# Cross-attention of a gated decoder stack: probabilities with keys on the partitions, from a pass that only finds row maxima

## The reference

```python
nx = _ln(x, g_ln2, b_ln2)
q = _heads(nx @ W_cq + b_cq, B)
k = _heads(img @ W_ck + b_ck, B)
v = _heads(img @ W_cv + b_cv, B)
s = jnp.einsum('bhqd,bhkd->bhqk', q, k) * SCALE
p = jax.nn.softmax(s, axis=-1)
co = _merge(einsum('bhqk,bhkd->bhqd', p, v), B) @ W_co + b_co
x = x + co
nx = _ln(x, g_ln3, b_ln3)
ff = jax.nn.gelu(nx @ W_ff1 + b_ff1, approximate=False) @ W_ff2 + b_ff2
x = x + ff
```

## Time and profile before

| | us |
|---|---|
| median of three runs | 491.4 |
| lowest, highest | 486.12, 491.94 |
| the profiled execution | 489.61 |
| its span, first to last instruction | 487.7 |
| mean granted TensorE clock of the profiled execution | 0.851 |

### The profile page before, as it was taken

How to read it: one execution, slowest core, us unless ns; L and a number is a source line. 1 busy time by engine, 2 the same in 40 slices (tenths; PEclk the granted TensorE clock), 3 DMA queues, 4 the chain that set the end, 5 groups by cost and what they waited for, 6 DMA issues and landing times.

```text
span 487.7 us, 6630 instructions
## 1 busy us (share of the span) xinstructions
PE 355.8 (73%) x2483; PEld 210.6 (43%) x2483; DVE 265.9 (55%) x675; ACT 201.7 (41%) x314; POOL 106.2 (22%) x144
## 2 busy tenths in 40 slices
PE   1987600996048899999998799987954998578810
PEld 1766500895024233333323476644643435456810
DVE  5245500232375998888831587536189566541157
ACT  2212200322022157777787377654442564725100
POOL 2000078000762351111110000000000235603163
PEclk9999555899566799999999599996975998989975
DMA  4493012111217466000000000007995476310232
GB/s 107 154 309 110 0 48 95 38 34 45 61 47 191 121 181 144 1 2 2 2 3 0 0 1 0 2 0 241 362 292 146 156 250 198 109 44 17 51 81 60
DMA packets 34002, 45.21 MB, mean 93 GB/s; under 512 B 4889, under 2 KB 19744, under 8 KB 33972
## 3 DMA queue, kind: packets, MB, share of 16 engines
q1 hardware_dynamic: 31156, 37.50, 26.2%
q0 software_dynamic: 2816, 7.31, 5.7%
HBM read 31.92 MB, written 12.71 MB: 92 GB/s over the span
## 4 chain that ended last, share of the span: by engine, by line
PE 59%; DVE 16%; issue 7%; ACT 6%; POOL 6%; DMA 3%; another core or an unknown queue 2%; SPq 1%; POOLq 0%; DVEq 0%; ACTq 0%
PE ps L1323 8%; PE ps L1520 6%; PE ps L1491 5%; PE ps L1508 5%; PE ps L1767 3%; PE ps L1438 3%; DVE mcol L1134 3%; PE ps L1450 3%; PE ps L1612 3%; POOL R L519 3%; PE ps L1793 2%; PE ps L1717 2%; POOL disp_d L514 2%; PE ps L1660 2%
## 5 line engine op out<-in xcount | busy, mean ns | idle before, releaser
L1134 DVE TENSOR_REDUCE mcol<-ps 128x1 f32<-128x512 f32 x128 | 80.3, 684 | 6.7 <-PE ps L1491 6.4
L686 ACT ACTIVATE R<-ps 128x1024 f32<-128x1024 f32 x64 | 62.6, 1020 | 25.2 <-PE ps L1508 24.3
L1323 PE MATMUL ps<-ident,R 128*77 128x128 f32 (+1 forms) x216 | 32.4, 289 | 27.4 <-DMA R<-disp_d 24.7
L1491 PE MATMUL ps<-R 72*128 72x512 bf16 x128 | 47.1, 399 | 1.0
L1323 PEld LDWEIGHTS ps<-ident,R 128*77 128x77 f32 (+1 forms) x216 | 25.3, 151 | 44.5 <-DMA R<-disp_d 25.1
L1508 PE MATMUL ps<-R 75*128 75x512 bf16 x128 | 37.6, 379 | 0.3 <-ACT R L686 0.2
L576 POOL DMA_INDIRECT R<-h_d,srow x16 | 16.0, 1002 | 84.3 <-DMA h_d<-ff 76.8
L1323 PE MATMUL ps<-ident,xn 128*128 128x128 f32 x48 | 12.9, 406 | 28.8 <-issue 18.0
L1520 PE MATMUL ps<-R,vaug 128*9 128x512 f32 x256 | 33.5, 595 | 0.6 <-ACT R L686 0.6
L1491 PEld LDWEIGHTS ps<-R 72*128 72x128 bf16 x128 | 12.8, 100 | 36.1 <-DVE mcol L1134 24.7
L1092 DVE TENSOR_SCALAR R<-ps,vcol 128x256 f32<-128x256 f32 x16 | 7.0, 479 | 38.4 <-PE ps L1438 38.4
(11 more groups left out here) (308 smaller groups left out, 695.6 us busy)
## 6 DMA issues: line engine op xcount, KB each, us to landing
R<-in_L_ffn_W_dram SPq DMA_DIRECT2D x1, 6144.0 KB, 19.8
h_d<-R SPq DMA_DIRECT2D x12, 256.0 KB, 2.9
q_d<-R SPq DMA_DIRECT2D x24, 96.0 KB, 2.0
R<-k_d SPq DMA_DIRECT2D x24, 96.0 KB
R<-q_d SPq DMA_DIRECT2D x8, 288.0 KB
R<-in_L_ffn_w_dram SPq DMA_DIRECT2D x1, 2048.0 KB, 11.5
h_d<-ff SPq DMA_DIRECT2D x6, 256.0 KB, 2.7
y_d<-R SPq DMA_DIRECT2D x10, 128.0 KB, 1.8
```

Source lines behind the costliest of these rows:

```text
L686: s.activation(probs[idx % 4], ps[:, 2 * (idx % 2):2 * (idx % 2) + 2, :].rearrange("p b t -> p (b t)"), ACT.Exp, scale=QK_SCALE).then_inc( ...
L1134: v.tensor_reduce(mcol[:, u, col:col + 1], bank(ring_bank("row", n)), AX.X, ALU.max).then_inc(s1_max, 1)
L1323: return m.transpose(dst, src, ident[0:k, 0:k])
L1491: m.matmul(bank(ring_bank("row", n)), Q9[0:KQ, b, h, t * P:(t + 1) * P], K9[0:KQ, b, h, :], start=True, stop=True).then_inc(s1_mm, 1)
```

## The change

Scores are computed twice. In pass one they have queries on the partitions as before, but only their maxima are taken (`cross_max`, one reduction a unit). The products of a unit are now cut to the 32 dimensions of their group of heads: two products of 32 contracted rows, on row groups 32·hg, into banks 4 and 5 or 6 and 7 in turn. Between units 1 to 10 stands an idle product of 256 columns, `spin(256)`. For each batch `split_maxima` turns the negated maxima into three bf16 parts, `max_rows` transposes them with an identity (four bf16 products), and ScalarE copies them to `cmrow`.

Pass two works in 8 quads, q = 4·b + j: head j of each of the four groups, all 512 queries of the batch. `cross_keys` makes four fp32 products, keys on the partitions and 512 queries in the columns, each on its own row group and into its own bank, and adds the negated maxima of the row with four bf16 products with a selector, `part_sel`. The pairs of banks are 0, 2, 0, 2 for the first two quads and then 4, 0, 2 in rotation. ScalarE takes the exponential straight from PSUM into `PT`, two banks at a time; `cross_values`, the copy, the output transposes and the division follow per quad, with the heads in another order (`across`). The 128 transposes of exponentials, the 32 copies and the 16 subtractions are gone.

The lists are interleaved anew. TensorE: units 0 to 10, maxima of batch 0, quad 0, units 11 and 12, quad 1, units 13 to 15, quad 2, values 0, maxima of batch 1, values 1, and then quads, values and output transposes in turn; projection 0 stands ahead of quad 7; the first feed-forward layer of batch 0 stands ahead of attention transposes and projection of batch 1. ScalarE: `evac_attnT(0, 1)` stands ahead of `std_of(3, 1, [0])`; in the end `evac_oT` and `evac_xT` of batch 0 stand ahead of `evac_attnT(1, 1)`, and two Gelus ahead of `evac_xT` of batch 1. GpSimd builds the selector and a bf16 identity behind its work for self-attention. W1 is loaded once the last values product of self-attention is done, W2 once the last one of cross-attention is. Bank numbers of the joints change with `at`.

The removed bodies of `cross_exp`, of `cross_values` and of the loops over units are those printed above; the rest of the core:

```diff
-        qcT = r1(16384 + 2048, 1024)
-        PT = [r1(8192 * b, 8192, J).rearrange("p (h t) -> p h t", h=NH) for b in range(B)]
-        PC = 8 * J
-        pc = [r1(16384 + PC * i, PC).rearrange("p (h j) -> p h j", h=8) for i in range(3)]
+        qcT = r1(22528, 1024)
+        PT = [r1(12288 + 2048 * i, 2048, J).rearrange("p (g t) -> p g t", g=4) for i in range(3)]
+        cmparts = r1(20480, 512).bitcast(BF16).rearrange("p (b t c) -> p b t c", b=B, t=TB)
+        cmrow = r1(20992, 512).bitcast(BF16).rearrange("p (b q) -> p b q", b=B)
+        part_sel = r1(21504, 2 * J).bitcast(BF16).rearrange("p (j n) -> p j n", j=4)
+        ident_b = r1(21664, P // 2).bitcast(BF16)
+        cmax = r1(21728, T * NH).rearrange("p (t h) -> p t h", t=T)
+        crest = r1(21856, TB * NH).rearrange("p (t g j) -> p t g j", t=TB, g=4)
+        sel_col = r1(21920, 4)
...
+        cross_order = [("nat", un) for un in range(11)] + [("max", 0), ("pair", 0), ("pair", 1)]
+        cross_order += [("nat", 11), ("nat", 12), ("pair", 2), ("pair", 3), ("nat", 13), ("nat", 14), ("nat", 15)]
+        cross_order += [("pair", 4), ("pair", 5), ("max", 1)] + [("pair", p) for p in range(6, 4 * HG)]
+        cross_done = {use: i + 1 for i, use in enumerate(cross_order)}
+        pair_bank = lambda p: (0, 2)[p % 2] if p < 4 else (4, 0, 2)[(p - 4) % 3]
+        score_bank = lambda un: 4 + 2 * (un % 2)
+        max_of = lambda un: un + 1 + un // T
+        parts_of = lambda b: (T + 1) * (b + 1)
...
-            sp.wait_ge(o_norm, 4 * HG)
+            sp.wait_ge(pv_mm, TB * UNITS)
             sp.dma_start(W1, a["L1_ffn_W1"].rearrange("e m h -> m e h")).then_inc(ld_W1, 16)
+            sp.wait_ge(c_pv, 2 * HG)
             sp.dma_start(W2, a["L1_ffn_W2"].rearrange("e (k f) m -> f (e k) m", f=P)).then_inc(ld_W2, 16)
...
-            pool.wait_ge(c_mm, 2 * T)
+            pool.wait_ge(part_wr[0], 64 * B)
+            pool.wait_ge(part_wr[1], 64 * (HG - 1) * B)
+            me.step(g.memset(r1(20480, 512), 0.0))
+            me.step(g.tensor_copy(ident_b, ident[:, :]))
+            me.link(g.memset(sel_col, 0.0))
+            for i in range(3):
+                for hg in range(HG):
+                    me.link(g.affine_select(out=sel_col, in_=sel_col, compare_op=ALU.not_equal, fill=1.0,
+                                            base=-(32 * hg + 4 * i), pattern=[[-1, 4]], channel_multiplier=1))
+            g.tensor_copy(part_sel, sel_col.unsqueeze(2).to_broadcast([P, 4, J])).then_inc(kbd_ready, 1)
+            pool.wait_ge(c_mm, len(cross_order))
...
-            evac_attnT(0, 0)
+            evac_attnT(0, 0, 0)
+            evac_attnT(0, 1, 1)
             std_of(3, 1, [0])
-            evac_attnT(0, 1)
...
+            def evac_max_rows(b):
+                act.wait_ge(c_mm, cross_done["max", b])
+                s.copy(cmrow[:, b, :], bank((0, 7)[b])).then_inc(c_row, 1)
+            def cross_exp(q, half):
+                act.wait_ge(c_mm, cross_done["pair", 2 * q + half])
+                if q >= 3 and half == 0:
+                    act.wait_ge(c_pv, q - 2)
+                bk = pair_bank(2 * q + half)
+                s.activation(PT[q % 3][:, 2 * half:2 * half + 2, :].rearrange("p g t -> p (g t)"),
+                             ps[0:J, bk:bk + 2, :].rearrange("p b t -> p (b t)"), ACT.Exp, scale=QK_SCALE).then_inc(c_exp, 1)
+            evac_max_rows(0)
+            for q in range(2 * HG):
+                cross_exp(q, 0)
+                if q >= 1:
+                    evac_oT(2 * HG + q - 1, c_pv, q)
+                cross_exp(q, 1)
+                if q == 2:
+                    evac_max_rows(1)
+                if q == 5:
+                    evac_attnT(1, 0, 7)
             std_of(4, 1, [0])
-            evac_attnT(1, 1)
+            evac_oT(4 * HG - 1, c_pv, 2 * HG)
+            evac_xT(4, V_LN3, [0], (4, 5))
+            evac_attnT(1, 1, 7)
...
-            evac_xT(4, V_LN3, [0])
             std_of(4, 1, [1])
-            for f in range(3):
+            for f in range(2):
                 gelu(0, f)
-            evac_xT(4, V_LN3, [1])
-            gelu(0, 3)
+            evac_xT(4, V_LN3, [1], (4, 5))
+            for f in range(2, 4):
...
+                heads = attn[:, b * TB:(b + 1) * TB, :].rearrange("p t (g j d) -> p t g j d", g=4, j=4)
+                v.tensor_tensor(heads[:, :, :, hg, :] if across else heads[:, :, hg, :, :],
...
-            for un in range(2 * T):
-                dve.wait_ge(c_mm, un + 1)
-                bk = 2 * (un % 2)
+            def cross_max(un):
+                t, half = un // 2, un % 2
+                dve.wait_ge(c_mm, cross_done["nat", un])
+                bk = score_bank(un)
                 sc = ps[:, bk:bk + 2, 0:4 * J].rearrange("p b (h j) -> p b h j", h=4)
...
+                v.tensor_reduce(cmax[:, t, 8 * half:8 * half + 8].rearrange("p (b h) -> p b h", b=2), sc, AX.X,
+                                ALU.max).then_inc(c_max, 1)
+            def split_maxima(b):
+                dve.wait_ge(kbd_ready, 2)
+                dve.wait_ge(c_max, max_of(T * (b + 1) - 1))
+                top = cmax[:, b * TB:(b + 1) * TB, :].rearrange("p t (g j) -> p t g j", g=4)
+                cols = cmparts[:, b].rearrange("p t (g c) -> p t g c", g=4)
+                me.link(v.tensor_scalar(cols[:, :, :, 0:4], top, -1.0, None, ALU.mult))
+                me.link(v.scalar_tensor_tensor(out=crest, in0=top, scalar=-1.0, in1=cols[:, :, :, 0:4], op0=ALU.mult,
+                                               op1=ALU.subtract))
+                me.link(v.tensor_copy(cols[:, :, :, 4:8], crest))
+                v.tensor_tensor(cols[:, :, :, 8:12], crest, cols[:, :, :, 4:8], ALU.subtract).then_inc(c_max, 1)
+            for un in range(T):
+                cross_max(un)
+            split_maxima(0)
+            for un in range(T, 2 * T):
+                cross_max(un)
+            split_maxima(1)
+            for j in range(HG):
+                normalize(2 * HG + j, j, 0, across=True)
+            normalize(3 * HG, 0, 1, across=True)
+            add_projection(1, 0, 6)
             stats_of_sum(1, 0)
-            for hg in range(2, HG):
-                normalize(3 * HG + hg, hg, 1)
+            normalize(3 * HG + 1, 1, 1, across=True)
             scale_of(xa, xn, 4, 0)
-            add_projection(1, 1)
+            for j in range(2, HG):
+                normalize(3 * HG + j, j, 1, across=True)
+            add_projection(1, 1, 6)
...
+            def group_rows(hg):
+                return slice(32 * hg, 32 * hg + 32)
             def cross_scores(un):
                 t, half = un // 2, un % 2
+                if un == 0:
+                    pe.wait_ge(qc_ready, 1)
+                elif un == T:
+                    pe.wait_ge(qc_ready, 2)
                 if un >= 2:
-                    pe.wait_ge(c_sub, un - 1)
-                else:
-                    pe.wait_ge(qc_ready, un + 1)
+                    pe.wait_ge(c_max, max_of(un - 2))
                 for j in range(2):
-                    h = 8 * half + 4 * j
-                    ins = m.matmul(ps[:, 2 * (un % 2) + j, 0:4 * J], qcT[:, t * P:(t + 1) * P],
-                                   kbd[:, t // TB, h:h + 4, :].rearrange("p h j -> p (h j)"), start=True, stop=True)
+                    hg = 2 * half + j
+                    ins = m.matmul(ps[:, score_bank(un) + j, 0:4 * J], qcT[group_rows(hg), t * P:(t + 1) * P],
+                                   kbd[group_rows(hg), t // TB, 4 * hg:4 * hg + 4, :].rearrange("p h j -> p (h j)"),
+                                   start=True, stop=True)
                 ins.then_inc(c_mm, 1)
...
+            def max_rows(b):
+                pe.wait_ge(c_max, parts_of(b))
+                if b == 0:
+                    pe.wait_ge(qc_ready, 2)
+                for s in range(TB):
+                    ins = m.matmul(ps[:, (0, 7)[b], s * P:(s + 1) * P], cmparts[:, b, s, :], ident_b, start=True, stop=True)
+                ins.then_inc(c_mm, 1)
+            def cross_keys(q):
+                b, j = q // HG, q % HG
+                if q == 1:
+                    pe.wait_ge(c_exp, 2)
+                elif q == 2:
+                    pe.wait_ge(c_max, max_of(2 * T - 2))
+                    pe.wait_ge(c_exp, 3)
+                elif q >= 3:
+                    pe.wait_ge(c_exp, 2 * q - 1)
+                banks = [pair_bank(2 * q + hg // 2) + hg % 2 for hg in range(HG)]
+                if q == 0:
+                    pe.wait_ge(c_row, 1)
+                for hg in range(HG):
+                    m.matmul(ps[0:J, banks[hg], :], kbd[group_rows(hg), b, 4 * hg + j, :],
+                             qcT[group_rows(hg), b * SEQ:(b + 1) * SEQ], start=True, stop=False)
+                pe.wait_ge(c_row, b + 1)
+                for hg in range(HG):
+                    ins = m.matmul(ps[0:J, banks[hg], :], part_sel[group_rows(hg), j, :], cmrow[group_rows(hg), b, :],
+                                   start=False, stop=True)
```

(61 more changed lines are left out.)

115 lines of the change are left out of this document (26 added, 89 removed).

## The result

The changed kernel takes 508.1 us (median of 4 runs, 506.5 to 508.7); the kernel before, run beside it, 490.3 us (4 runs, 486.1 to 491.9). The ratio is 1.037, interval 1.030 to 1.045: slower by some 18 us, and outside the range that the prediction gave. The profiled execution has a span of 504.6 us (before 487.7) and a mean granted clock of 0.814. Some executions of these kernels fall into a slower state with a lower granted clock; ratios and intervals leave them out.

The account below looks back on a forecast made before the run. It took the kernel to be TensorE bound, 1.91 us a unit. The sum - 3.3 + 3.1 + 1.5 + 0.8 = + 2.1 us on the median of 491.4 gave 493 us, with an 80% range of 483 to 504.

Parts of the forecast that it names:

- the prediction's walk: Queue-by-queue timing from entry to the second feed-forward product: start at 344.6 us against 347.93 before, 3.3 us earlier.
- the clock terms: Low-clock additions: + 3.1 us for the first layer, + 1.5 before the second, + 0.8 for quad 2's holes.
- The entry: Before the scores: ScalarE's second attention copy ahead of the variance wait starts scores at 277.9 us, 1.2 earlier.
- Row groups overlap: Scores: products on separate row groups run side by side, a quad 1.35 us; the no-overlap rival, 518 us, had chance 0.08.
- The unit at full clock: Pass one: TensorE needs 0.73 us a unit and VectorE 0.83, so VectorE bounds it.
- a change of tiling mode: Pass one, counter-argument: full-row idle products drain the array; at 0.1 us each, units take 0.93 us, ending 1 us later.
- The hole in quad 2: TensorE idles twice around quad 2, 1.5 and 2.4 us, waiting on round trips and ScalarE's queue.
- The exit: Last output transposes at 327.3 us to second feed-forward product at 344.6; first layer now precedes the second half's projection.
- the stage gains nothing that matters: Whole stage: the longer exit chain cancels the gain, a loss of 1 to 3 us; this was the forecast, chance 0.56.
- W1, W2 and GpSimd: The earlier W1 load, W2's new wait and GpSimd's sixteen set-up operations were all priced at nothing.
- the sum's term for the clock in the stage: Quad 2's holes may drop the clock: at most 3.1 us at one in four, booked as 0.8 us.
- the clock stays low in the stage: Rival: partly idle array and holes keep 1.2 GHz for five to seven quads, + 14 to + 20, 507 to 513; chance 0.12.

Follow-up runs that it names:

- g2: Changed kernel without idle products; third to eleventh units of pass one issue two extra unread products on the other two row groups; ratio 1.018.
- g3: f4 with g2's extra products on the other two row groups in place of the idle products in pass one; ratio 0.989.
- e5: Kernel before with only ScalarE's second attention copy moved ahead of its wait for the variance; ratio 1.001.
- e2: Changed kernel without the 256-column idle products between the units of pass one; ratio 1.022.
- e4: Changed kernel with the old exit order: second half's attention transposes and projection ahead of the first layer, ScalarE's order to match; ratio 1.021.
- f1: Changed kernel with the edits of e3, e4 and e6 together; ratio 1.004 to the kernel before.
- f4_w1_late: f4 with the W1 load waiting again for the last division of cross-attention, as in the kernel before; ratio 0.998.
- e1: Changed kernel with pass one's score products contracting all 128 rows again instead of 32; ratio 1.028.
- e3: Changed kernel with two 512-column idle products between units of pass one instead of one of 256; ratio 1.019.
- e6: Changed kernel with ScalarE's copy of the second batch's maxima moved ahead of the second exponential of quad 1; ratio 1.034.
- h1: g1 with every unit up to the eleventh on row groups 0 and 1 only, which alters the output; ratio 1.042.
- g1: Changed kernel without idle products; third to eleventh units of pass one issue their two row-tiled products twice, copies unread; ratio 1.018.
- g4: f4 with eleven more 512-column idle products in the holes of the exit; ratio 0.993.
- f4: f1 plus last output copy before Sqrt table load, last divisions before scaling, first output transposes before second values; 1.000. Variants: no idle products, late W1.

## Why the prediction was wrong, point by point

On the scale of the profiled executions, the prediction's walk beside the changed kernel and beside g2 and g3:

| step | forecast | changed | g2 | g3 |
|---|---|---|---|---|
| scores start | 277.9 | 278.00 | 277.97 | 278.51 |
| first quad | 290.6 | 294.45 | 289.67 | 290.23 |
| fourth quad | 306.0 | 312.06 | 304.54 | 302.37 |
| eighth quad | 319.6 | 329.65 | 319.32 | 316.65 |
| last output transposes | 327.3 | 337.02 | 326.70 | 322.97 |
| first layer | 329.2 | 339.68 | 329.27 | 328.13 |
| second layer | 340.9, 344.0 with + 3.1 | 353.59 | 343.25 | 333.19 |
| second feed-forward product | 344.6, 350.0 with the clock terms | 359.14 | 348.86 | 336.73 |

**Right.** *The queues.* With the clock up in pass one (g2), every step of the walk up to the first layer came within 1.5 us, and the second feed-forward product at 348.9 where the walk with its clock terms said 350.0. *The entry*: 278.00 for 277.9, with 0.8 to 0.9 us of gain for 1.2 (e5) that can't be seen in the time. *Row groups overlap*: the eight fp32 records of a quad take 0.92 us (303.96 to 304.88), 3.7 times less than 8 x 0.43; the whole quad 1.24 us to the next block, forecast 1.35. *The unit at full clock*: 0.93 us (280.25 to 281.18) where the forecast had 0.83, bound by VectorE. The prediction names 0.93 too, for a change of tiling mode at 0.1 us each, but that figure was met by luck: the products take 0.72 us, not 0.52 to 0.62, and take 0.7 in e2 as well, where no full-row product stands between; the idle product takes the other 0.21. *The hole in quad 2*: 1.3 and 2.1 us for 1.5 and 2.4. *The exit*: 22.1 us from the last transposes, forecast 17.3 and 4.6 for the clock. Its order was rightly seen as a loss, and e4 and f1 price it at 6.3 and 4.7 us; I booked it as "the stage gains nothing that matters", where it is a quarter to a third of the slowdown. *W1, W2 and GpSimd* at nothing: f4_w1_late bears out W1; W2 and GpSimd were not tried by themselves.

**Wrong: the clock in the stage.** The step that failed is the sum's term for the clock in the stage: 0.8 us, all of it for the holes in quad 2, and nothing for pass one behind its first two units, which was costed at the full clock at 0.83 us a unit. The runs show a unit of 1.65 us at the low clock, and 9.7 us by the last output transposes. The rival "the clock stays low in the stage" had a chance of 0.12, with 507 to 513 us, and its signs came: four quads at 2.0 us and reductions 1.65 us apart. That the median of 508 lies in its range is partly luck, though: it had 14 to 20 us for low-clock quads alone, where pass one and the quads together lost 10, and nothing for the 5.7 us at the end. The chain of the miss, in microseconds of the changed kernel over the forecast: first quad + 3.9; first to fourth quad 17.6 for 15.4, + 2.2; fourth to eighth 17.6 for 13.6, + 4.0; behind that - 0.3. That is 9.7 at the last output transposes, less the 0.8 booked, and + 0.2 in the exit: 9.1 of the 14.8 us by which the span of 504.6 misses the forecast of 489.8 (487.7 + 2.1). g2, where four row groups work in pass one, has its last output transposes 10.3 us sooner. Two causes lie in this. The first two steps, + 3.9 and + 2.2, are the low clock that pass one brings about. The + 4.0 is the dip behind the hole ahead of the fourth quad, the very place of the 0.8 us: 3.1 us at one in four, and it came. It does not hang on pass one alone. Behind the same 2.1 us hole it lasts ten microseconds in the changed kernel, in e2 and in e1, which had full rows and the full clock, and 3 to 4 in e3 and g2; with a shorter hole it is 3 to 4 us in e6 and absent in f1. What sets its length was not settled.

Two arguments carried the error. First, as evidence against the rival I took the values block at 299.40, nine output columns wide and at full clock. But it uses all four column groups and its neighbours were full-array transposes; pass one uses two row groups of four and only a short full-row product between. Nothing in the trace of before was like that, and I let the nearest row decide the chance rather than hold it as unknown. Second, I looked for the cause of a low clock in holes, since both dips of before stood behind holes. Pass one has a gap of only 0.1 us a unit by the prediction's own figures, so it seemed safe. e1, g2 and h1 show that a busy TensorE is not enough.

A smaller one: the idle product was costed at full clock, 0.11 us; at the low clock it is 0.39 with its tail and, as e2 against the changed kernel shows, 0.3 us a unit in the pace.

**Not foreseen: 5.7 us behind the second feed-forward product.** From its start to the end it is 145.5 us, and 139.8 in the trace of before. Much of this need not be the change's: the kernel before shows 142.9 and 143.5 in two other traces. Where a trace of before was taken on the same chip, the changed kernel has 144.7 beside 142.9, and h1 144.6 beside 143.5: 1 to 2 us. In g1, g3, g4 and e1 to e4, on the chips where the kernel before is at 483 us, it is 137.7 to 138.8, in g2, on the same chip as g3, 141.7. Within these kernels it is 140.7 in f1 and 143.6 to 143.9 in the three f4 ones. Low-clock stretches lie at other places there in each trace (the changed kernel: 371 to 388, 419 to 423, 429 to 436, 449 to 456). TensorE runs the same 1097 products there and is busy for 96.1 us in the changed kernel, 91.3 in the trace of before and 93.2 in its two others, so the clock has a part in it; but g3, with 93.1, has 137.7 us where the kernel before with 93.2 has 142.9. The early W1 load is not the reason (f4_w1_late). What moves it was not settled, and whether the 1 to 2 us belong to the change stays open.

## What to carry to other kernels

When a stage is packed with products on part of the array, ask of each stretch how many row groups work, not only whether TensorE is busy: in h1 two of four left it at half its clock for 17 us while the busy share read 100%. Price a reordering of the joins behind a stage at both clock levels and beside the old order in the same units; 4.7 to 6.3 us were lost there, and undoing it gave them back with no other change. If the array must be kept at full clock, products that put the idle row groups to work are cheaper than idle products in between: 0.86 us a unit against 1.25.

## What the runs showed of the hardware that I had not expected

- The granted clock stayed at 0.50 from 272 to 312 us in h1, with TensorE busy 5.00 of 5.00 us in three stretches in a row on two row groups, and at 1.00 in g2 with four row groups and 3.10 of 5.00 us busy.
- A short idle product was worse than none: at 256 columns it did not hold the clock and cost 0.3 us a unit; two of 512 columns held it, in five traces.
- At full clock, a unit's four records on two row groups took 0.72 us to the next product, where the forecast had 0.52 for two pairs side by side; with two more products on the other two groups a unit was still 0.86 us, VectorE's own pace.
- The kernel before itself starts its second feed-forward product at 347.9, 345.6 and 344.5 us in three traces. Between the first two the whole 2.4 us lie ahead of the end of self-attention, and the rest takes 81.1 us in both; in the third the low stretch at 271 to 281 us is missing, and it takes 77.1. So two traces of the same kernel can stand 4 us apart within the part that was changed, where their low-clock stretches fall differently.
